# Where the column sum of a batch norm is formed: on VectorE ahead of one matmul, or by ten matmuls on TensorE

## The reference

```python
conv_out = jax.nn.relu(agg @ W_conv + b_conv)      # agg: mean of the neighbours' rows
...                                                 # h_attn: attention over the nodes
return _batchnorm(conv_out + h_attn + h, norm2_g, norm2_b)

def _batchnorm(x, g, b):
    mu = jnp.mean(x, axis=0)
    var = jnp.mean((x - mu) ** 2, axis=0)
    return (x - mu) * jax.lax.rsqrt(var + EPS) * g + b
```

## Time and profile before

| | us |
|---|---|
| median of 3 runs | 1472.05 |
| lowest, highest | 1471.31, 1476.17 |
| the profiled execution | 1476.17 |
| its span in the profile | 1474.4 |
| TensorE busy in it | 1316.5 (89%) |
| VectorE busy in it | 578.9 (39%) |

### The profile page before, as it was taken

One profiled execution on the slowest core, in us unless ns is written; L12 is line 12 of the kernel. 1 busy time (PEld: TensorE's weight loads), 2 busy tenths in 40 slices (PEclk: granted clock), 3 DMA queues, 4 the chain that ended last, 5 costly groups with the idle time before them and its releaser, 6 DMA issues.

```text
span 1474.4 us, 17744 instructions
## 1 busy us (share of the span) xinstructions
PE 1316.5 (89%) x5780; PEld 832.7 (56%) x5781; DVE 578.9 (39%) x1554; ACT 465.9 (32%) x1008; POOL 206.9 (14%) x207
## 2 busy tenths in 40 slices
PE   4899999999998999899889999888399999669698
PEld 2554585565565554577557767556164576334376
DVE  9999632111234431111111111111473234755883
ACT  5899532221122100111111111111122322226783
POOL 1000000000000072000110010111543000102460
PEclk9999999999999999999999999999699899869999
DMA  9000000000201132511643115605450000200001
GB/s 235 38 1 1 2 2 0 1 1 0 86 29 52 64 87 90 202 43 37 213 141 108 43 54 190 212 25 207 108 175 14 1 2 1 93 0 0 1 29 43
DMA packets 45297, 96.92 MB, mean 66 GB/s; under 512 B 8495, under 2 KB 10857, under 8 KB 44065
## 3 DMA queue, kind: packets, MB, share of 16 engines
q1 hardware_dynamic: 27205, 68.70, 13.9%
q0 software_dynamic: 10560, 16.23, 4.1%
q10 hardware_dynamic: 7452, 10.97, 2.0%
HBM read 79.72 MB, written 16.10 MB: 65 GB/s over the span
## 4 chain that ended last, share of the span: by engine, by line
PE 79%; DVE 10%; issue 4%; ACT 3%; DMA 1%; ACTq 1%; POOL 1%; DVEq 0%; POOLq 0%
PE psum L418 42%; PE psum L1774 13%; PE psum L1829 7%; PE psum L1754 4%; PE psum L1948 3%; PE psum L446 2%; PE psum L1854 1%; PE psum L1891 1%; DVE sb_hT_conv L1368 1%; PE psum L1841 1%; PE psum L1886 1%; PE psum L1804 1%; ACT sb_htok L783 1%; DVE sb_blk L1167 1%; DVE sb_stats L426 1%
## 5 line engine op out<-in xcount | busy, mean ns | idle before, releaser
L418 PE MATMUL psum<-sb_w_reg,sb_blk 128*128 128x256 f32 x896 | 215.3, 396 | 6.1 <-issue 6.1
L418 PEld LDWEIGHTS psum<-sb_w_reg,sb_blk 128*128 128x128 f32 x896 | 176.2, 200 | 41.2 <-issue 17.5
L1774 PE MATMUL psum<-sb_z_reg_r,sb_hT_conv_r 125*125 125x512 f32 x400 | 170.2, 425 | 0.2 <-issue 0.2
L418 PE MATMUL psum<-sb_w_reg,sb_hT_conv 128*125 128x512 f32 (+1 forms) x376 | 168.5, 597 | 1.8 <-ACT sb_hT_conv L1054 1.8
L1774 PE MATMUL psum<-sb_htok_r,sb_hT_conv_r 125*125 125x512 f32 x300 | 117.9, 393 | 0.0
L1164 DVE TENSOR_TENSOR sb_blk<-sb_blk,psum 128x256 f32<-128x256 f32 x56 | 23.6, 422 | 232.3 <-ACT sb_blk L757 232.3
L418 PEld LDWEIGHTS psum<-sb_w_reg,sb_hT_conv 128*125 128x125 f32 (+1 forms) x376 | 68.7, 189 | 79.2 <-issue 76.0
L1829 PE MATMUL psum<-sb_w_reg,sb_blk 128*128 128x512 f32 x224 | 108.2, 605 | 2.2
L418 PE MATMUL psum<-sb_hT_conv,sb_w_reg 128*128 128x416 f32 (+2 forms) x304 | 102.3, 496 | 0.7 <-ACT sb_hT_conv L452 0.7
L736 ACT CAST sb_hT_conv_r<-sb_a_reg 125x625 fp32r<-125x625 f32 x80 | 56.1, 715 | 115.0 <-PE psum L1774 114.9
L1774 PEld LDWEIGHTS psum<-sb_z_reg_r,sb_hT_conv_r 125*125 125x125 f32 x400 | 75.5, 189 | 25.1 <-issue 7.6
(11 more groups left out here) (379 smaller groups left out, 1766.1 us busy)
## 6 DMA issues: line engine op xcount, KB each, us to landing
sb_hT_conv<-w_expert SPq DMA_DIRECT2D x7, 2048.0 KB, 10.8
sb_w_reg<-w_expert SPq DMA_DIRECT2D x6, 2048.0 KB, 10.5
sb_hT_conv<-w_expert SPq DMA_DIRECT2D x7, 1024.0 KB, 12.8
slot_outs<-sb_blk ACTq DMA_DIRECT2D x28, 256.0 KB
sb_w_reg<-w_expert SPq DMA_DIRECT2D x6, 1024.0 KB
sb_w_reg<-w_gnn SPq DMA_DIRECT2D x1, 4096.0 KB, 43.8
sb_w_reg<-w_qkv SPq DMA_DIRECT2D x1, 3072.0 KB, 19.4
slot_outs<-sb_blk ACTq DMA_DIRECT2D x1, 2560.0 KB, 12.6
```

The lines of the kernel that those rows point to most:

```text
L418: ins = e.matmul(out, l, r, start=(n == 0), stop=(n == len(pairs) - 1))
L1774: ins = e.matmul(psum[0:TP, b, :], counts_at(l, 2 * i + n // NT)[:, s % HALF_T, :], z[s], start=(n == 0), stop=(n == len(pairs) - 1))
```

## The change

The eight additions into `y_sum` on VectorE go, and with them the matmul of `mean_w` with `y_sum`. Instead TensorE multiplies `mean_w` with each of the ten tiles of y and accumulates in bank 0, each matmul behind a wait for its tile's `y_ready`. Seven of these stand between the neighbour sums of tile 8 and tile 9, three behind the sum of tile 9. `y_ready` ends at 10, and SyncE waits for 10 instead of 11.

```diff
-        y_sum = blk[0:TP, 1536:2048]
...
-            e.wait_ge(y_ready, NT + 1)
+            e.wait_ge(y_ready, NT)
             e.dma_start(w_reg[:, 0, KD * D:], a["w_last"][:, KD * D:]).then_inc(ld_last, 16)
...
             for i in range(NT):
-
-                if i == 2:
-                    e.wait_ge(y_ready, 2)
-                    e.tensor_tensor(y_sum, htok[:, 0, :], htok[:, 1, :], ALU.add).then_inc(v_own, v.up())
-                elif i > 2:
-                    e.wait_ge(v_own, v.n)
-                    e.wait_ge(y_ready, i)
-                    e.tensor_tensor(y_sum, y_sum, htok[:, i - 1, :], ALU.add).then_inc(
-                        *((y_ready, 1) if i == NT - 1 else (v_own, v.up())))
                 if i > SUMS_IN_TURNS:
                     vec_convolved(e, i)
...
-            for i in range(SUMS_IN_TURNS + 1, NT):
+            for i in range(SUMS_IN_TURNS + 1, NT - 1):
                 pe_conv_sum(e, flag, i)
-            e.wait_ge(y_ready, NT)
-            e.matmul(psum[0:TP, 0, :], mean_w, y_sum, start=True, stop=False)
-            e.wait_ge(y_ready, NT + 1)
-            e.matmul(psum[0:TP, 0, :], mean_w, htok[:, NT - 1, :], start=False, stop=True).then_inc(mean_mm, 1)
+            for i in range(NT):
+                if i == SUMS_IN_TURNS + 1:
+                    pe_conv_sum(e, flag, NT - 1)
+                e.wait_ge(y_ready, i + 1)
+                ins = e.matmul(psum[0:TP, 0, :], mean_w, htok[:, i, :], start=(i == 0), stop=(i == NT - 1))
+            ins.then_inc(mean_mm, 1)
```

## The result

The changed kernel takes 1484.0 us (median of 5 runs, 1479.16 to 1489.40), the kernel before in the same set 1472.05 us (1470.53 to 1476.17). The ratio is 1.0068, 95% interval 1.0044 to 1.0093: slower, as forecast, but by some 10 us by that ratio (6.5 to 13.7) where 5.9 was forecast, and outside the range of 1474.3 to 1481.0. Wherever a difference in us is given beside a ratio from here on, it is the ratio's part of the kernel before's median in the same set. The changed kernel's profiled execution took 1478.98 us with a span of 1477.2 us; the one of before 1476.17 and 1474.4 us.

What follows compares the result with a forecast made beforehand. It took TensorE alone to bound the stretch until tile 9's sum ends, then VectorE until the last mean matmul. Median 1472.05 plus 6.0 for seven uncovered matmuls, less 0.2 for the clock, other terms 0: 1477.9 us, range 1474.3 to 1481.0.

Steps and rivals of the forecast that it cites:

- VectorE's relief at 0: Around the last neighbour sums: removing eight `y_sum` additions, 5.5 us of VectorE work, gains 0, as no waiter shows.
- `y_sum`'s matmul and the third matmul behind tile 9's sum at 0: Behind tile 9's sum: removing one matmul and having three instead of two costs 0, covered by VectorE's 2.29 us.
- Seven matmuls at 0.858 us, uncovered, 6.0 us: Between tile 8's and tile 9's sums: fourteen records of 0.429 us on gapless TensorE add 6.0 us.
- The DMA shift at 0: SyncE's loads from `w_last` on fire 6.0 us later, but with some 30 us of cover: cost 0.
- The fall of the clock at the variance: Variance matmuls behind the mean: shorter TensorE idle makes the half-clock stretch less likely, giving back up to 1.7 us.
- So against the median I take only the mechanical part: Final sum: 6.0 us put on the median 1472.05, less 0.2 us for the clock fall's lower chance, 1477.9 us.
- the only term of this size: Clock fall as the only term seen of the size of the profiled execution's 4.12 us over the median.
- that the matmuls are nearly free: First rival, ahead of tile 9's sum: seven matmuls cost as little as rounded neighbours or find a gap, +1.6 us; chance 0.08.
- the second: Rival: last layer's first matmuls get full clock one stretch later, total 7.6 us, 1479.7 us; chance 0.12.
- That the added work keeps the clock up behind 1279: Third rival, through the end of the batch norm: 10.3 us back against 6.0, so 4.3 us faster, 1467.8; chance 0.03.

Runs made afterwards that it cites:

- experiment 4: Kernel before without the eight `y_sum` additions, two mean matmuls (tiles 8 and 9), so the mean leaves out tiles 0 to 7: 1563.96 us, ratio 1.0599.
- experiment 6: Changed kernel with all ten mean matmuls behind tile 9's sum: ratio 1.0045; kernel before with four behind it, none ahead: ratio 0.9996.
- the double dose: Changed kernel with each of the seven mean matmuls ahead of tile 9's sum issued once more into an unused bank: ratio 1.0108.
- the null: The kernel before again under another name, nothing changed: 1475.41 us, ratio 0.9997.
- the changed kernel again: The changed kernel rerun unaltered, in a later set: 1483.13 us, ratio 1.0051 against the kernel before.
- experiment 3: Kernel before plus the seven mean matmuls ahead of tile 9's sum, results overwritten; VectorE still forms `y_sum`: ratio 1.0039.

## Why the prediction was wrong

- VectorE's relief at 0: right. The stretch is 17.40 us without any of the additions (experiment 4).
- `y_sum`'s matmul and the third matmul behind tile 9's sum at 0: right (experiment 6, and 0.6 us of idle time left). One reading beside it was off: the attention add that starts 1.5 us behind its sum in the earlier trace rows is tile 8's own, at 1260.64; tile 7's starts more than 3 us behind its sum.
- Seven matmuls at 0.858 us, uncovered, 6.0 us: right to 0.03 us in both profiles of the changed kernel, and linear to the double dose.
- The DMA shift at 0: right; the last layer starts as far behind the subtraction as in the null, 44.7 us (1270.40 to 1315.07, and 1268.41 to 1313.07).
- The fall of the clock at the variance credited to the change, "1482.2 if it stays", 1480.5 if it goes: wrong as a credit. It is 8.86 us in the null and 10.56 in the changed kernel's second profile, so one pair of profiles told of the executions, not of the kernels. The size, 1.7, was close: 10.42 against 8.86 is 1.56. In the final figure it weighed only 0.2 us.
- "So against the median I take only the mechanical part": this is the step that failed. I held the profiled 1476.17 us for a slow execution, 4.12 us over what the kernel does, and put the 6.0 on a median of three, 1472.05. Over 100 runs the kernel before has its median at 1475.6. The profiled execution was the ordinary one and the median of three the odd one. Nor is a fall of the clock at the variance "the only term of this size": the start of tile 7's sum alone lies 9.5 us apart between profiles. The sum that the prediction made first, 1476.17 + 6.0 = 1482.2, lies 0.9 us from the 1483.1 of the second set and 1.8 from the first set's 1484.0.
- The rivals: that the matmuls are nearly free fell with 0.429 us a record; the second, that the clock of the last layer's first matmuls rises later, was not seen: the 48 matmuls take 18.92 and 18.55 us in the changed kernel, 20.13 and 18.52 in the kernel before. That its 7.6 us are close to the measured 7.5 is luck. That the added work keeps the clock up behind 1279 fell, since the changed kernel's transposes still take 1.08 us and its clock is 0.50 there as before.
- The range inherited the low base, and allowed 1.5 us upward for the scatter of a median where that base was 3.5 us off. On the base of 1475.6 the forecast would have been 1481.4 and the upper end 1484.5, with 1484.0 inside.

What stays open is the 1 to 2 us between the stretch's 6.0 and the whole's 7.5 (4.6 to 10.6), and the larger distance in the first set and in the double dose. The base accounts for 3.5 of the 6.1 us between the forecast 1477.9 and 1484.0; 1 us is the first set's 1484.0 over the later 1483.1, and the remaining 1.7 us are this surplus and the 0.2 us that I took off for the clock.

## What to carry to other kernels

Where the engine that gets the work is busy without a gap and the engine that is relieved is waited for nowhere, moving work costs its full time; read this from the chain and the busy share of the stretch, not from the engines' totals. The same matmuls are free in the one place where TensorE waits for VectorE anyway, up to that wait's length. When a profiled execution and a median of three differ by less than the spread of single runs, neither is the base: put the effect on both and let the range hold both. And a clock state seen in one profile of each kernel belongs to the executions until a second profile of each shows it again.

## What the runs showed that I had not expected

The time at which identical code reaches tile 7's sum varies between executions from 1245.87 us (the changed kernel again) to 1255.34 (experiment 3), so much of this kernel's spread is made ahead of the stretch that changed. Not all: what lies behind that start takes 224.6 and 221.0 us in the two profiles of the kernel before. A kernel's run time can hang on a branch on data 145 us further on: leaving out part of a mean cost 88 us in a selection that had been quick.
